# Expert results scattered in token order by GpSimd, and read back by plain loads, in the second expert stage

## The reference, cut to what matters

```
x = x + attention_a(layernorm(x))      # 16 heads, latent width 32, rotary, causal
x = x + ffn(layernorm(x))              # first expert stage
x = x + attention_b(layernorm(x))      # 16 heads of width 8, causal
x = x + ffn(layernorm(x))              # second expert stage

def ffn(flat):                         # E = 8 experts, F = 512, top 2 for each token
    logits = flat @ gate_w + gate_b
    topv, topi = top_k(logits, 2);  topw = softmax(topv)
    final = sum over the two chosen experts e of
            topw_e * (gelu(flat @ w1[e] + b1[e]) @ w2[e] + b2[e])
```

## Time and profile before

| | us |
|---|---|
| median of three runs (lowest, highest) | 1364.26 (1359.78, 1368.37) |
| profiled execution | 1355.24 |
| its span in the trace | 1351.5 |
| busy PE, DVE, ACT, POOL | 1043.1, 811.1, 658.5, 876.9 |
| mean granted TensorE clock, share of full speed | 0.861 |
| granted clock in the second expert loop (1130 to 1262 us) | 0.97 |

### The profile page before, as it was taken

One profiled execution on the slowest core, in us unless ns is written; L12 is line 12 of the kernel. 1 busy time (PEld: TensorE's weight loads), 2 busy tenths in 40 slices (PEclk: granted clock), 3 DMA queues, 4 the chain that ended last, 5 costly groups with the idle time before them and its releaser, 6 DMA issues.

```text
span 1351.5 us, 31386 instructions
## 1 busy us (share of the span) xinstructions
PE 1043.1 (77%) x11163; PEld 806.5 (60%) x11164; DVE 811.1 (60%) x2006; ACT 658.5 (49%) x1214; POOL 876.9 (65%) x1173
## 2 busy tenths in 40 slices
PE   2599999999999565999546888898998367999300
PEld 1466676677666345999524555565565257999300
DVE  3577778777775383565316666666666483555222
ACT  0266676676665202555345566656675103555100
POOL 0489989989986165555256787768564085554476
PEclk9699999999998656999868899979899558999755
DMA  9000000000000001223200000000000002323122
GB/s 234 1 2 2 2 10 10 7 5 10 10 2 10 32 0 43 79 76 74 47 18 16 17 24 25 9 17 25 9 10 9 24 5 54 79 78 70 54 76 76
DMA packets 56247, 45.70 MB, mean 34 GB/s; under 512 B 13571, under 2 KB 48259, under 8 KB 56131
## 3 DMA queue, kind: packets, MB, share of 16 engines
q0 software_dynamic: 9088, 18.63, 6.1%
q1 hardware_dynamic: 39378, 22.44, 5.8%
q10 hardware_dynamic: 7664, 3.04, 1.0%
HBM read 27.57 MB, written 16.52 MB: 33 GB/s over the span
## 4 chain that ended last, share of the span: by engine, by line
PE 58%; DVE 18%; POOL 9%; issue 5%; ACT 4%; DMA 3%; another core or an unknown queue 1%; ACTq 1%; DVEq 1%; POOLq 0%
PE PS L1616 10%; PE PS L1329 6%; POOL got L642 5%; PE PS L1431 5%; PE PS L1398 5%; PE PS L1331 4%; PE PS L1330 4%; PE PS L1380 3%; DVE M L839 2%; PE PS L1411 2%; PE PS L1387 2%; DVE X L1087 2%; DMA b_cols<-in_L_ffn_b_dram 2%; DVE stats L705 1%; PE PS L1581 1%
## 5 line engine op out<-in xcount | busy, mean ns | idle before, releaser
L539 POOL TENSOR_SCALAR_AFFINE_SELECT PT<-PT 128x256 f32<-128x256 f32 x512 | 219.1, 451 | 116.6 <-ACT PT L1127 115.4
L1127 ACT ACTIVATE PT<-PS 128x768 f32<-128x768 f32 x256 | 206.7, 807 | 134.6 <-PE PS L1526 80.2
L671 POOL DMA_INDIRECT xg<-normed,source x156 | 150.1, 962 | 118.5 <-PE PS L1594 81.6
L642 POOL DMA_INDIRECT got<-expert_rows,slot_of x128 | 121.9, 953 | 80.6 <-DMA expert_rows<-y_rows 46.3
L1255 ACT ACTIVATE hid<-PS,b_cols 128x256 f32<-128x256 f32 x312 | 122.3, 475 | 98.6 <-PE PS L1331 77.2
L1616 PE MATMUL PS<-W,hid 128*128 x1248 | 156.1, 279 | 4.5 <-issue 2.2
L1616 PEld LDWEIGHTS PS<-W,hid 128*128 128x128 f32 x1248 | 149.4, 195 | 5.6 <-issue 5.6
L1380 PE MATMUL PS<-causal_b,ident_b 128*128 128x256 bf16 x512 | 103.6, 287 | 40.8 <-DVE q_aug L912 29.1
L1398 PE MATMUL PS<-PT,v_aug 128*32 128x256 f32 (+1 forms) x2048 | 116.3, 348 | 10.2 <-POOL PT L539 10.1
L1087 DVE SCALAR_TENSOR_TENSOR X<-got,weight,X 128x128 f32<-128x128 f32 x128 | 56.4, 446 | 75.9 <-DMA got<-expert_rows,slot_of 66.1
L1329 PE MATMUL PS<-xg_hi,w_hi 128*128 128x256 f32 x312 | 97.1, 311 | 2.2 <-issue 2.2
(11 more groups left out here) (265 smaller groups left out, 3234.8 us busy)
## 6 DMA issues: line engine op xcount, KB each, us to landing
expert_rows<-y_rows SPq DMA_DIRECT2D x78, 128.0 KB
normed<-xn SPq DMA_DIRECT2D x16, 256.0 KB, 2.3
xg<-normed,source POOLq DMA_INDIRECT x156
W<-in_L_ffn_w_dram SPq DMA_DIRECT2D x1, 2048.0 KB, 16.2
got<-expert_rows,slot_of POOLq DMA_INDIRECT x128, 2.5
out_dram<-X SPq DMA_DIRECT2D x8, 256.0 KB
b_rows<-in_L_ffn_b_dram SPq DMA_DIRECT2D x2, 512.0 KB, 3.5
X<-in_L_attn_a_x_dram ACTq DMA_DIRECT2D x2, 256.0 KB, 4.4
```

Source lines behind the costliest of these rows:

```text
L539: ins = nc.gpsimd.affine_select(out=diagonal, in_=diagonal, pattern=[[0, 2], [1, P]], compare_op=ALU.is_ge, fill=0.0, base=0, channel_mult ...
L642: nc.gpsimd.indirect_dma_start(out=got[:, k, :], out_offset=None, in_=rows_out, in_offset=bass.IndirectOffsetOnAxis(ap=slot_of[:, which * ...
L671: nc.gpsimd.indirect_dma_start(out=xg[:, i % 4, b_, :], out_offset=None, in_=normed, in_offset=bass.IndirectOffsetOnAxis(ap=source[:, k:k ...
L1127: s.activation(PT[:, unit % 2, 2 * pair:2 * pair + 2, :], PS[:, 4:6, 0:3 * P], ACT.Exp).then_inc(m["exp_done"], 1)
```

## The change

In the second expert stage only, `expert_rows` and its 39 stores are not used. A new DRAM buffer, `spread2`, has one row for each (token, choice) in token order, 8192 rows, and behind them one row of its own for each padding row. VectorE works out `target`, the row to which each row of each block goes, in four more small operations on 128x78 elements: one ahead of the signal `slots_ready`, three behind it. GpSimd's loop over tiles issues, behind the two gathers of tile i, two indirect scatters of tile i - 6 from `y_rows` to `spread2` (BEHIND = 6), and the last six tiles' scatters behind the loop: 156 indirect DMAs in place of 78. The ring `y_rows` is given free by the scatters' landing: each tile counts two.

When all scatters have landed, SyncE loads the 8 chunks, 512 KB each with 1 KB in a piece (both choices of a token are neighbours), into two buffers in turn: `got`, and the ring `xg`, which the loop needs no longer. From chunk 2 on a load waits for the additions of the chunk two before. VectorE makes the same 64 additions, in each chunk first the four of choice 0 and then the four of choice 1. The output stores are issued by ScalarE's queue. The 64 gathers of L642 go. The constant table grows by 78 columns (128 x 78 x 4 B = 40 KB more in the first loads).

```diff
+BEHIND = 6
+    spread = {n: nc.dram_tensor(f"spread{n}", [2 * T + BLOCKS * P, D], F32, kind="Internal").ap() for n in SPREAD}
+    spread_tiles = {n: ap[0:2 * T, :].rearrange("(t p k) d -> p t (k d)", p=P, k=2) for n, ap in spread.items()}
...
+        last_rows = (got, xg[:, :, :, :].rearrange("p r b d -> p (r b) d"))
...
@@ sync
+            def all_spread(n):
+                for r in range(4):
+                    sp.wait_ge(moe_sems[n][f"stored{r}"], 16 * RB * len(range(r, TILES, 4)))
+            def load(n, c, dst, signal):
+                sp.dma_start(dst.rearrange("p (t k) d -> p t (k d)", k=2), spread_tiles[n][:, c * CT:(c + 1) * CT, :]).then_inc(moe_sems[n][signal], 16)
...
-                tile_slots(sp, store)
-            for c in range(NCH):
-                sp.wait_ge(moe_sems["2"]["got_used"], 2 * CT * (c + 1))
-                sp.dma_start(out_tiles[:, c * CT:(c + 1) * CT, :], X[:, c * CT:(c + 1) * CT, :]).then_inc(stored, 16)
+                if e_ in SPREAD:
+                    all_spread(e_)
+                    load(e_, 0, got[:, :, :], "loaded0")
+                else:
+                    tile_slots(sp, store)
+            me = moe_sems["2"]
+            for c in range(1, NCH):
+                if c > 1:
+                    sp.wait_ge(me["got_used"], 2 * CT * (c - 1))
+                load("2", c, last_rows[c % 2], f"loaded{c % 2}")
...
@@ gpsimd, gather_rows
+                def send(i):
+                    pool.wait_ge(m["y_ready"], i + 1)
+                    for b_ in range(RB):
+                        k = i * RB + b_
+                        nc.gpsimd.indirect_dma_start(
+                            out=spread[n], out_offset=bass.IndirectOffsetOnAxis(ap=target[:, k:k + 1], axis=0),
+                            in_=y_rows[:, i % 4, b_, :], in_offset=None).then_inc(m[f"stored{i % 4}"], 16)
...
+                    if n in SPREAD and i >= BEHIND:
+                        if i == BEHIND:
+                            pool.wait_ge(m["targets_ready"], 1)
+                        send(i - BEHIND)
+                if n in SPREAD:
+                    for i in range(TILES - BEHIND, TILES):
+                        send(i)
...
-            for c in range(NCH):
-                gather_results("2", c)
...
@@ vector
+                if n in SPREAD:
+                    own.did(v.tensor_scalar(second[:, :], bank[1][:, 0:BLOCKS], 0.0, None, ALU.is_gt))
...
+                if n in SPREAD:
+                    own.did(v.scalar_tensor_tensor(empty[:, :], source_f[:, 1, :], 0.0, con("aside"), ALU.is_lt, ALU.mult))
+                    own.then(v.scalar_tensor_tensor(second[:, :], source_f[:, 1, :], 2.0, second[:, :], ALU.mult, ALU.add))
+                    v.tensor_tensor(target[:, :], second[:, :], empty[:, :], ALU.add).then_inc(m["targets_ready"], 1)
...
-                        dve.wait_ge(m[f"stored{r}"], stores_before(i, r))
+                        dve.wait_ge(m[f"stored{r}"], stores_before(i, r) * (RB if n in SPREAD else 1))
...
+            def add_all_rows(n):
+                m = moe_sems[n]
+                for c in range(NCH):
+                    dve.wait_ge(m[f"loaded{c % 2}"], 16 * (c // 2 + 1))
+                    for which in range(2):
+                        for t in range(CT):
+                            if which:
+                                dve.wait_ge(m["got_used"], c * (2 * CT) + t + 1)
+                            v.scalar_tensor_tensor(X[:, c * CT + t, :], last_rows[c % 2][:, 2 * t + which, :], weight[which][:, c * CT + t:c * CT + t + 1],
+                                                   X[:, c * CT + t, :], ALU.mult, ALU.add).then_inc(m["got_used"], 1)
...
@@ scalar
+            for c in range(NCH):
+                act.wait_ge(moe_sems["2"]["got_used"], 2 * CT * (c + 1))
+                act.dma_start(out_tiles[:, c * CT:(c + 1) * CT, :], X[:, c * CT:(c + 1) * CT, :]).then_inc(stored, 16)
+            act.wait_ge(stored, 16 * NCH)
```

More of the change, by code:

```diff
@@ L33 @@
 BLOCKS = TILES * RB
+SPREAD = ("2",)
 EPS = 1e-5
@@ L39 @@
 _at = 0
-for _name, _n in (("ident", P), ("cos", S), ("sin", S), ("block_no", BLOCKS), ("lane_no", P), ("token_no", NT), ("prefer", E),
+for _name, _n in (("ident", P), ("cos", S), ("sin", S), ("block_no", BLOCKS), ("lane_no", P), ("token_no", NT), ("prefer", E), ("aside", BLOCKS),
                   ("stack", 2), ("one24", 1),
@@ L80, in constants @@
     put("one24", (p % L == 3 * HD).astype(np.float32)[:, None])
+    put("aside", 2 * T + 2 + p[:, None] + P * np.arange(BLOCKS, dtype=np.float32))
     put("prefer", np.broadcast_to(E - np.arange(E, dtype=np.float32), (P, E)))
@@ L413, in program @@
             source = sb("source", [P, BLOCKS], I32, moe)
+            second = sb("second", [P, BLOCKS], F32, moe)
+            empty = sb("empty", [P, BLOCKS], F32, moe)
+            target = sb("target", [P, BLOCKS], I32, moe)
             emap_f = sb("emap_f", [1, TILES, E], F32, moe)
@@ L466, in program @@
         moe_sems = {n: {k: sem(f"m{n}_{k}") for k in (
-            "gap_ready", "exp_ready", "mask_ready", "rank_ready", "hot_ready", "blocks_ready", "block_hot_ready", "hot_used", "slots_ready",
+            "gap_ready", "exp_ready", "mask_ready", "rank_ready", "hot_ready", "blocks_ready", "block_hot_ready", "hot_used", "slots_ready", "targets_ready", "loaded0", "loaded1",
             "row0", "row1", "row2", "row3", "turned", "turned_hi", "split", "staged", "up_ready", "gelu_ready",
@@ L673, in gather_rows @@
                             in_offset=bass.IndirectOffsetOnAxis(ap=source[:, k:k + 1], axis=0)).then_inc(m[f"row{i % 4}"], 16)
-                for r in range(4):
-                    pool.wait_ge(m[f"stored{r}"], 16 * len(range(r, TILES, 4)))
+                    if n in SPREAD and i >= BEHIND:
[5 more added lines that the diff above has]
+                        send(i)
+                else:
+                    for r in range(4):
+                        pool.wait_ge(m[f"stored{r}"], 16 * len(range(r, TILES, 4)))
             pool.wait_ge(rest_loaded, 16 * N_REST)
@@ L1082, in add_expert_rows @@
                     t, which = c * CT + k // 2, k % 2
-                    dve.wait_ge(m[f"got{k}"], c * 16 + 16)
+                    if n in SPREAD:
+                        dve.wait_ge(m["loaded0"], c * 16 + 16)
+                    else:
+                        dve.wait_ge(m[f"got{k}"], c * 16 + 16)
                     if which:
@@ L1095, in _ @@
             experts("2")
-            for c in range(NCH):
-                add_expert_rows("2", c, range(2 * CT))
+            add_all_rows("2")
         @block.scalar
```

## The result

The changed kernel takes 1401.8 us (median of 4 runs, 1390.7 to 1405.0) where the kernel before takes 1362.0 (4 runs, 1349.6 to 1368.4): a ratio of 1.029, interval 1.019 to 1.039. The forecast was 1360, within 1340 to 1386. The change makes the kernel slower by some 40 us, and the forecast was wrong. The profiled execution, the fastest of the four, took 1390.68 us with a span of 1388.0, 36.5 more than the 1351.5 before.

The account below looks back on a forecast made before the run. PE was taken to bound the expert loop, POOL's indirect-DMA pace the tail. The stretch behind the loop shrinks from 84.2 to 30.8 us, the loop grows by 48.6: -4.7 us, 1364.26 becomes 1359.6, say 1360; range 1340 to 1386.

Parts of the forecast that it names:

- Does anything hold POOL up?: Second expert loop: the added waits are covered and cost nothing; the last tile's scatter has 2 us of cover.
- not POOL's: Start of the second expert loop: the wait ahead of the first `y_rows` isn't due to POOL and stays.
- POOL needs 4 x 1.26 = 5.04 us for a tile, POOL becomes the bound: Second expert loop: four issues a tile, each 0.96 us and 0.30 to the next, outlast PE's 3.43 us.
- POOL at 9 tenths or more: Expected sign in the changed loop's profile: POOL this busy from 1131 to 1310, with 142 issues at 1.24 to 1.28 us.
- (a): Loop: VectorE holds up POOL's issues; if all 142 take 1.12 us, 23 us more, 1383; chance 0.13.
- (b): Loop: the scatter is dearer in itself; at 1.46 us 39 us more, 1399; chance 0.11.
- (c): Loop: PE's clock falls; at half clock about 6.8 us a tile, 58 us more, 1418; chance 0.04.
- (d): Loop: the scatter is cheaper; at 0.6 us 28 us less, 1332; chance 0.14.
- (e): Tail not shortened: loads at 201 GB/s or late; 4 to 8 us, 1364 to 1368; within the forecast's 0.58.
- size for the tail: Behind the loop: from the last scatter's landing through loads, additions and output stores to the span's end, 35.0 us.
- The change trades 64 issues behind the loop for 78 in it: Whole change: same engine, little hidden; behind the loop 84.2 us become 30.8, the loop grows by 48.6 us.
- The slack of 53 us: Loop before the change: POOL idles some 53 us, which is all there is to win.

Follow-up runs that it names:

- the two-deep start: The kernel before with GpSimd gathering two tiles ahead in place of four, in both expert stages: 1339.7 us beside 1352.5, ratio 0.989.
- the bursts: The kernel before with single rows of 2, 4, 6, 8, 12 and 16 more indirect gathers: 1439.5 us beside 1361.0; with 16-row gathers 1431.8 us.

## Why the prediction was wrong

**The step that failed is the one under "Does anything hold POOL up?"**, with its answer "nothing". The accounting: the first scatter starts at 1130.73 (forecast 1131.8), 141 issues follow, and POOL waits 20 more times for `y_rows`, 44 us in all; of that 0.3 us each would have passed anyway, so 38 us are lost. With 5.9 us for dearer issues, and less the 1.1 us of the earlier start, that is the 42.8 us by which the last scatter is late. The forecast followed the waits that the code has and found each of them covered, with PE at its own speed. It had the evidence against this in hand: it named the wait ahead of 1130.6 "not POOL's", though it stood behind 14 issues of POOL in a row. The only other long row that met a busy PE, at the start of the first expert stage, has the same stop (6.6 us); the tail's 64 in a row had PE idle beside them.

**"POOL needs 4 x 1.26 = 5.04 us for a tile, POOL becomes the bound"**: the price of a scatter was right, 1.00 us for 0.96, and the gather's 0.98. POOL and PE now hold each other up: row and rest make 6.25 us. One of the forecast's signs was set wrong in any case: "POOL at 9 tenths or more" doesn't fit issues of 0.96 us every 1.26, which are 76% busy.

**Rivals.** (a) and (b), VectorE and a dear scatter, came in small: (0.99 - 0.96) x 142 = 4 us, and some late issues. (c) named the clock, and it fell to 0.84; but it is not what makes a tile 6.25 us, since the kernel with more gathers takes as long at 0.90, and three issues a tile cost 1.15 us a tile at 0.98. (d) didn't happen. (e) didn't either: loads took 3.9 to 5.4 us (median 4.8) for the forecast 3.5, eight additions 2.20 us for 3.16, and it is luck that the two errors cancelled. The forecast's own size for the tail was right to 1.6 us.

**"The change trades 64 issues behind the loop for 78 in it"** was the right view with the wrong exchange rate. An issue behind the loop costs 1.25 us, with TensorE idle. One in the loop costs nothing only if POOL's rest stays long enough. With the third issue a tile costs 1.15 us more, with the fourth 1.67 more. The slack of 53 us that the forecast saw in POOL's loop is made of the rests in which TensorE's signals come through.

What stays open is how GpSimd's issue reaches TensorE. The runs show which issues do it, not the path. Nor do they give a rule for when: the signals come out later the longer the row, but some come in its middle, and the row of eight at the two-deep start made no stop. The ends of matmuls are modelled in the profile, so a matmul that really ended late would look just like a late signal. And but for the two-deep start each experiment is one run, while runs of the kernel before spread over 16 to 19 us; the conclusions rest on what the traces show, and of the times only on differences well above that (38 to 84 us for the kernels with added indirect gathers).

## What to carry to other kernels

Before moving indirect DMAs from an idle stretch under a busy TensorE, count how many GpSimd would issue in a row: pairs with a rest of 1.2 us cost nothing here, three in a row cost about what they take, and four and more mostly stopped TensorE, except with a rest of about 2 us, which cost more still. Look in a trace for "remote" waits or dispatch gaps of PE behind rows of indirect issues, the first fill of a ring above all, and don't fill a ring deeper than the loop needs: that edit of two lines gave 1.1%. A wait whose releaser the profile can't name is a question, and not a constant that stays when the work around it changes.

## What the runs showed of the hardware

- Indirect DMAs issued in a row by GpSimd delay TensorE's signals until 0.9 us (row of three), 1.7 us (row of eight) to 3.2 us (row of 16) after the last issue, with some coming through in the middle of the long rows, and, from 5.4 to 7.5 us into the bursts, TensorE's dispatch too, down to a matmul in 0.7 to 2.1 us. VectorE's signals came through in the same rows: in the long burst `xg_lo` ended at 1261.87 and PE's next matmul began at 1262.12.
- 16 plain DMAs in a row by GpSimd took 8.85 us, 0.55 each, and delayed nothing. An indirect one took 0.85 us with 16 rows, 0.95 with 128, and 1.00 as a scatter to DRAM, with 0.30 us to the next.
- 24 memsets in a row on GpSimd held one cast of VectorE for 9.76 us, which else takes 0.43; 8, 12, 16 and 32 of them held it for 2.3, 4.0, 6.0 and 13.5 us.
- A load of 512 KB from DRAM by SP beside others took 3.9 to 5.4 us from issue to landing, median 4.8.
